# A four-layer gated transformer on one core: the next norm's centred input summed in PSUM at the ends of the attention layers, and the mixture's gate moved into its one-hots

## The reference, cut to what matters

```
x = x + tanh(g_xattn[0]) * L0_xattn(layernorm(x), ctx)      # differential attention, output Wp, bias bp
x = x + tanh(g_ffn[0])   * L0_ffn(layernorm(x))             # 8 experts, top 1, gate = softmax probability
x = x + tanh(g_xattn[1]) * L1_xattn(layernorm(x), ctx)      # linear attention, output Wo, bias bo
x = x + tanh(g_ffn[1])   * L1_ffn(layernorm(x))             # token-shift mixing: sigmoid(r) * (relu(k)^2 W_v)
x = x + tanh(g_xattn[2]) * L2_xattn(layernorm(x), ctx)      # masked softmax attention
x = x + tanh(g_ffn[2])   * L2_ffn(layernorm(x))             # shared expert + 8 routed, top 2
x = x + tanh(g_xattn[3]) * L3_xattn(layernorm(x), ctx)      # softmax attention, rows masked at the end
x = x + tanh(g_ffn[3])   * L3_ffn(layernorm(x))             # sparse heads + dense causal heads
```

## Time and profile before

| what | value |
|---|---|
| median of 3 runs | 517.68 us (516.72 to 518.56) |
| profiled execution, its own time | 518.73 us |
| its span in the trace | 516.6 us |
| PE busy | 454.9 us, 88% of the span |
| DVE, ACT, POOL busy | 277.6, 231.3, 94.7 us |
| chain that ended last | PE 67%, DVE 17%, ACT 9%, nothing shown 4% |
| mean granted TensorE clock | 0.973 of full |

### The profile page before, as it was taken

One profiled execution on the slowest core, in us unless ns is written; L12 is line 12 of the kernel. 1 busy time (PEld: TensorE's weight loads), 2 busy tenths in 40 slices (PEclk: granted clock), 3 DMA queues, 4 the chain that ended last, 5 costly groups with the idle time before them and its releaser, 6 DMA issues.

```text
span 516.6 us, 6960 instructions
## 1 busy us (share of the span) xinstructions
PE 454.9 (88%) x2690; PEld 257.6 (50%) x2690; DVE 277.6 (54%) x567; ACT 231.3 (45%) x447; POOL 94.7 (18%) x87
## 2 busy tenths in 40 slices
PE   5889999889898887787888998889879979989996
PEld 2334443463773332576644774433346465566563
DVE  1566774344225446587216663546595568357451
ACT  3345565320331465534443335445664554547261
POOL 3000000140601002244000000003355314152300
PEclk9899999979999999899979999999997999999999
DMA  8500000530000000000000002001001101011000
GB/s 351 242 2 1 1 1 1 194 120 0 0 1 1 2 0 0 1 1 2 0 0 2 0 1 81 1 0 22 7 15 20 22 1 22 3 20 22 20 1 22
DMA packets 4594, 15.54 MB, mean 30 GB/s; under 512 B 1361, under 2 KB 1618, under 8 KB 4050
## 3 DMA queue, kind: packets, MB, share of 16 engines
q1 hardware_dynamic: 4562, 15.10, 8.7%
HBM read 12.73 MB, written 0.52 MB: 26 GB/s over the span
## 4 chain that ended last, share of the span: by engine, by line
PE 67%; DVE 17%; ACT 9%; issue 4%; POOL 1%; DMA 1%; SPq 0%; DVEq 0%; POOLq 0%
PE PS L503 58%; PE PS L1201 2%; DVE mxd L2285 2%; PE PS L736 2%; ACT xc L1407 1%; DVE mx L1846 1%; DVE wmoe L1839 1%; ACT xc L1408 1%; DVE keys L1993 1%; POOL wmoe L2510 1%; PE PS L574 1%; DMA cst<-const_dram 1%; DVE yb L2323 1%; DVE hp L1797 1%; ACT wmoe L1699 1%
## 5 line engine op out<-in xcount | busy, mean ns | idle before, releaser
L503 PE MATMUL PS<-PTB,keys 128*64 128x128 f32 (+4 forms) x416 | 46.1, 401 | 0.1
L1711 ACT COPY PTB<-PS 128x768 f32<-128x768 f32 (+1 forms) x24 | 20.9, 872 | 34.6 <-PE PS L1201 34.3
L1993 DVE TENSOR_REDUCE keys<-PS 128x9 f32<-128x693 f32 x32 | 26.6, 874 | 10.8 <-PE PS L503 10.8
L503 PE MATMUL PS<-keys,PTB 32*128 32x231 f32 (+2 forms) x384 | 29.6, 348 | 3.0 <-DVE keys L1968 1.6
L503 PEld LDWEIGHTS PS<-PTB,keys 128*64 128x64 f32 (+3 forms) x416 | 22.5, 148 | 17.9 <-issue 14.1
L503 PE MATMUL PS<-x,cst 128*128 128x512 f32 x32 | 19.5, 711 | 13.4 <-DMA cst<-const_dram 5.9
L2510 POOL TENSOR_TENSOR wmoe<-wmoe,mx 128x616 f32<-128x616 f32 x16 | 19.5, 1216 | 63.1 <-DVE mx L1848 63.1
L2528 POOL TENSOR_TENSOR den<-den,cst 128x1024 f32<-128x1024 f32 x7 | 16.9, 2421 | 76.4 <-DMA den<-wmoe 76.4
L503 PEld LDWEIGHTS PS<-keys,PTB 32*128 32x128 f32 (+1 forms) x384 | 21.2, 190 | 17.7 <-issue 12.8
L1532 ACT ACTIVATE PT<-PS 116x512 f32<-116x512 f32 (+1 forms) x32 | 17.4, 597 | 23.5 <-PE PS L503 23.5
L503 PE MATMUL PS<-wmoe 64*128 64x512 f32 (+3 forms) x128 | 24.1, 474 | 4.2 <-ACT mask L1699 3.1
(11 more groups left out here) (346 smaller groups left out, 976.5 us busy)
## 6 DMA issues: line engine op xcount, KB each, us to landing
wmoe<-w_dram SPq DMA_DIRECT2D x2, 2048.0 KB, 11.8
den<-wmoe SPq DMA_DIRECT2D x28, 64.0 KB, 2.3
wa<-wa_dram SPq DMA_DIRECT2D x4, 256.0 KB, 5.2
wlate<-ew_dram SPq DMA_DIRECT2D x2, 512.0 KB, 4.6
wd<-wd_dram SPq DMA_DIRECT2D x1, 1024.0 KB, 8.4
wlate<-wm_dram SPq DMA_DIRECT2D x1, 1024.0 KB, 4.7
cst<-const_dram SPq DMA_DIRECT2D x1, 738.0 KB, 6.5
cst<-const_dram SPq DMA_DIRECT2D x1, 670.5 KB, 4.6
```

The costliest lines, as they stand in the source:

```text
L503: return nc.tensor.matmul(o, l, r, start=start, stop=stop, skip_group_check=True)
L1711: nc.scalar.copy(PTR[n % 2][:, :, 0:width], PS[:, 4:6, 0:width]).then_inc(S("d_turned"), 1)
L1993: last = v.tensor_reduce(mxn[:, 2 * half + t, :].rearrange("p (g r) -> p g r", r=32)[:, :, 12:15], PS[:, 0:NG, t * 256:t * 256 + GK].rearr ...
```

## The change

The sum of the old x and the gated projection is formed inside the centring product. For six norms, (1, half 1), (3, both), (5, half 1) and (7, both), `ln_centre` is replaced by two products into one bank: `join_x` multiplies the old x by `center` and leaves the sum open, and `join_att` adds the product of `att` with a matrix `WC` that holds the output matrix, centred over its output features and multiplied by the gate. What the output bias contributes is a column `CENTRED_BIAS`, which ACT adds inside the square and DVE inside the scale; in layer 3 POOL adds it (masked) to x ahead of time, the mask is applied when `att` is placed, and the residual is one DVE operation that reads the projection's bank. The old path (projection, bias on ACT, add on DVE) stays for x itself, behind the join. The four `WC` matrices are made on DVE, three operations each, the first in `gates` of layer 0 and three in the expert loop, and PE centres three bias columns with one-column products.

The mixture's gate is multiplied with tanh(g_ffn[0]) in one 128x8 operation and then into every one-hot, so that `moe_add` is one DVE operation in place of two. Several orders are rewritten: in `between` on PE, ACT and DVE, at the end of `attention3`, and at the beginning of `final_layer`. Five `keep_clock` groups are gone.

```diff
--- before.py
+++ after.py
@@ banks and numbering @@
-BETWEEN = [("query", 0), ("den", 0), ("num", 0), ("project", 0), ("query", 1), ("k", 0), ("den", 1), ("num", 1),
...
+BETWEEN = [("query", 0), ("den", 0), ("num", 0), ("project", 0), ("k", 0), ("query", 1), ("r", 0), ("den", 1),
...
+        WC = [wa0[:, 0, :]] + [ctxf[:, 128 * n:128 * n + 128] for n in range(3)]
@@ PE @@
+            def join_x(i, b):
+
+                if i > 1:
+                    pe.wait_ge(S(f"x_ready_{b}"), i - 1)
+                mm(PS[:, centre_bank(i, b), :], C("center"), xb[b], stop=False)
+
+            def join_att(i, b):
+                mm(PS[:, centre_bank(i, b), :], WC[i // 2], att[:, b, :], start=False).then_inc(S(f"ln_centered_{b}"), 1)
@@ PE, end of layer 0 @@
                 ln_variance(1, 0)
                 keep_clock(2, 512, 512)
                 turn(1)
-                keep_clock(2, 512)
+                pe.wait_ge(S("centred"), CENTRED["first"])
+                join_x(1, 1)
                 project(1)
-                keep_clock(2, 512, 512)
-                pe.wait_ge(S("st_y_placed"), B)
@@ PE, attention of layer 2 @@
                 ln_centre(i + 1, 0)
                 step()
+                join_x(i + 1, 1)
                 ln_variance(i + 1, 0)
@@ PE, attention3 @@
                 for u in range(NU3):
+                    if u == 3:
+                        turn(0)
                     turned_scores(u)
                     if u + 1 < NU3:
                         scores(u + 1, 1)
+                    if u == 3:
+                        pe.wait_ge(S("st_att_done"), FIRST["att_done"] + 1)
+                        join_att(7, 0)
                     if u > 0:
                         turn_sums(u - 1)
                     if u + 1 < NU3:
                         turn_max(u + 1)
                     if u + 2 < NU3:
                         scores(u + 2, 0)
+                    if u == 2:
+                        pe.wait_ge(S("l3_set"), 8 + 2)
+                        join_x(7, 0)
                     if u == 3:
-                        turn(0)
-                        keep_clock(ROW_BANKS[0], 512)
-                        project(0)
+                        project3(0)
                     weigh(u)
-                ln_centre(7, 0)
+                ln_variance(7, 0)
                 turn_sums(NU3 - 1)
-                ln_variance(7, 0)
+                pe.wait_ge(S("l3_set"), 8 + 4)
+                join_x(7, 1)
                 turn(1)
-                keep_clock(KEY_BANKS[0], 512)
-                project(1)
+
+            def project3(b):
+                mm(PS[:, PROJECT_BANKS[b], :], wa3[:, 3, :], att[:, b, :]).then_inc(S("st_projected"), 1)
@@ PE, moe @@
                 for b in range(B):
-                    if b == 0:
-                        ln_centre(1, 1)
-                    else:
+                    if b == 1:
                         ln_variance(1, 1)
@@ PE, between @@
                 lin_sums(0)
+                join_x(3, 0)
                 combine(6, 1)
                 combine(7, 1)
+                pe.wait_ge(S("lin_att"), 1)
+                join_att(3, 0)
+                ln_centre(2, 1)
+                ln_variance(3, 0)
                 lin_project(0)
-                ln_centre(2, 1)
-                ln_centre(3, 0)
                 ln_variance(2, 1)
-                ln_variance(3, 0)
-                keep_clock(5, 512)
+                arrived(pe, "wf1")
+                pe.wait_ge(S("lin_y"), 1)
+                mixed(0, 1, 4)
                 lin_query(1)
-                arrived(pe, "wf1")
-                mixed(0, 1, 4)
+                mixed(0, 0, 0)
                 lin_sums(1)
-                mixed(0, 0, 0)
                 mix_values(0, 1)
+                join_x(3, 1)
+                pe.wait_ge(S("lin_att"), 2)
+                join_att(3, 1)
                 lin_project(1)
                 ln_centre(4, 0)
-                ln_centre(3, 1)
+                ln_variance(3, 1)
                 ln_variance(4, 0)
-                ln_variance(3, 1)
                 pe.wait_ge(S("at_k_placed"), 1)
                 query2(0, 0, 4)
                 query2(0, 1, 5)
+                pe.wait_ge(S("lin_y"), 2)
                 mixed(1, 1, 6)
@@ PE, final_layer @@
                 prepare(0)
-                pe.wait_ge(S("st_y_placed"), FIRST["y_placed"] + B)
                 pe.wait_ge(S("pool_set"), POOL_SET["swap"])
+                pe.wait_ge(S("st_att_done"), FIRST["att_done"] + B)
                 for j in (1, 0):
                     mm(PS[:, 2 + j, :], wswap[j], h[0]).then_inc(S("d_swapped"), 1)
+                join_att(7, 1)
+                project3(1)
                 prepare(1)
-                ln_centre(7, 1)
+                ln_variance(7, 1)
                 router(0)
-                ln_variance(7, 1)
                 scores(0)
+                pe.wait_ge(S("x_ready_1"), 7)
                 tokens(0)
@@ ACT @@
             def ln_squares(i, b):
                 act.wait_ge(S(f"ln_centered_{b}"), i + 1)
-                A_(sq[:, b, :], PS[:, centre_bank(i, b), :], ACT.Square).then_inc(S(f"ln_sq_{b}"), 1)
+                at = CENTRED_BIAS.get((i, b))
+                plus = {} if at is None else dict(bias=small[:, at:at + 1])
+                A_(sq[:, b, :], PS[:, centre_bank(i, b), :], ACT.Square, **plus).then_inc(S(f"ln_sq_{b}"), 1)
@@ ACT, between @@
                 lin_shares(0)
+                ln_squares(3, 0)
+                ln_squares(2, 1)
+                ln_root(3, 0)
                 lin_project(0)
-                ln_squares(2, 1)
-                ln_squares(3, 0)
                 ln_root(2, 1)
-                ln_root(3, 0)
-                lin_shares(1)
                 act.preload_act_table_set(TANHS)
                 mix_gate(0, 0)
                 act.preload_act_table_set(ROOTS)
+                lin_shares(1)
+                ln_squares(3, 1)
+                ln_squares(4, 0)
+                ln_root(3, 1)
+                ln_root(4, 0)
                 lin_project(1)
-                ln_squares(4, 0)
-                ln_squares(3, 1)
-                ln_root(4, 0)
-                ln_root(3, 1)
                 place2(0, 0, 4)
@@ DVE @@
+                    last = v.scalar_tensor_tensor(h[b], centred_x, small[:, at:at + 1], xc[:, b, :], ALU.add, ALU.mult)
+                last.then_inc(S(f"ln_h_{b}"), 1)
+
+            def centred(n, w, gate):
+
+                link(v.tensor_reduce(small[:, n:n + 1], w, AX.X, ALU.add))
+                link(v.tensor_scalar(small[:, n:n + 1], small[:, n:n + 1], -1.0 / D, None, ALU.mult))
+                v.tensor_scalar(WC[n], w, small[:, n:n + 1], tg[:, gate:gate + 1], ALU.add, ALU.mult).then_inc(S("centred"), 1)
@@ DVE, attention3 @@
                 def place(b):
                     dve.wait_ge(S("st_turned"), FIRST["turned"] + b + 1)
-                    v.tensor_copy(att[:, b, :], PS[:, MAX_BANK, :]).then_inc(S("st_att_done"), 1)
+                    v.tensor_tensor(att[:, b, :], PS[:, MAX_BANK, :], mask3f[:, b * T:(b + 1) * T],
+                                    ALU.mult).then_inc(S("st_att_done"), 1)
 
                 def add(b):
-                    dve.wait_ge(S("st_y_placed"), FIRST["y_placed"] + b + 1)
-                    link(v.tensor_tensor(yb[:, b, :], yb[:, b, :], mask3f[:, b * T:(b + 1) * T], ALU.mult))
-                    residual(b, 3)
+                    dve.wait_ge(S("st_projected"), FIRST["projected"] + b + 1)
+                    dve.wait_ge(S("l3_set"), 8 + 2 * (b + 1))
+                    v.scalar_tensor_tensor(xb[b], PS[:, PROJECT_BANKS[b], :], tg[:, 3:4], xb[b], ALU.mult,
+                                           ALU.add).then_inc(S(f"x_ready_{b}"), 1)
...
                 add(0)
                 take(NU3 - 1)
+                ln_scale(7, 0)
                 place(1)
-                ln_scale(7, 0)
                 add(1)
@@ DVE, start, moe and between @@
+                dve.wait_ge(S("gates"), 1)
+                dve.wait_ge(S("lam_dots"), 2)
+                v.tensor_scalar(small[:, 8:9], PS[:, 4, 400:401], tg[:, 0:1], None, ALU.mult)
+                link(v.tensor_scalar(r8t[:, 6, :], r8t[:, 6, :], tg[:, 4:5], None, ALU.mult))
...
+                    if 1 <= e <= 3:
+                        centred(e, (wa1, wa2, wa3)[e - 1][:, 3, :], e)
+                    elif e == 4:
+                        dve.wait_ge(S("moe_slots"), 3)
+                        v.tensor_scalar(small[:, 9:10], PS[:, 3, 256:257], tg[:, 1:2], None, ALU.mult)
+                        v.tensor_scalar(small[:, 10:11], PS[:, 3, 257:258], tg[:, 2:3], None, ALU.mult)
+                        v.tensor_scalar(small[:, 11:12], small[:, 13:14], tg[:, 3:4], None, ALU.mult).then_inc(S("centred"), 1)
-                v.tensor_scalar(GC[b][e % 2], destb[:, b * T:(b + 1) * T], C("slotid")[:, e:e + 1], None,
-                                ALU.is_equal).then_inc(S("moe_GT"), 1)
+                tokens = slice(b * T, (b + 1) * T)
```

(21 more changed lines are left out.)

60 lines of the change are left out of this document (37 added, 23 removed).

## The result

The changed kernel takes 522.77 us in the median of 20 executions (517.78 to 527.82), the kernel before 518.5 in the median of 20 (516.72 to 521.66). That is 4.3 us or 0.8% between the medians. The ratios in this document leave out executions that took over 1.5% more than the fastest of their kernel (5 of the 20 of the change), and the median of what is left is called trimmed. The trimmed median of the change is 521.35, its ratio 1.006 with a 95% interval of 1.0037 to 1.0082: slower by 0.6%. The forecast was 517.4, with a range of 514.7 to 520.1. The profiled execution is one of the slower ones of the 20, 526.37 us by its own time at a mean clock of 0.953, where the 20 together had 0.961.

A forecast was written before the change was run, and what follows sets the result against it. PE was taken to bound the kernel (busy 454.9 of 516.6 us), so edits count only where PE waits. Terms +0.6 - 1.94 + 0 + 1.84 - 0.24 - 0.5 = -0.24 took the median from 517.68 to 517.4, range 514.7 to 520.1.

The forecast's parts named there:

- Start of layer 0, +0.6: Start of layer 0: an added small DVE operation and `centred(0)` ahead of the reductions cost +0.6 us (0.2 to 1.1).
- the other +0.17: Start of layer 0: one more small DVE operation ahead of the eight at 14.91 costs +0.17 us with its gap.
- The half-clock rival: Ahead of layer 2's queries: 2.86 us of PE idle time brings half clock, price 1.5 to 3 us, time 519.5; chance 0.22.
- the sign that it named: The page's slice at 194 to 200 us shows a clock below 0.8.
- End of layer 0, -1.94: End of layer 0, norm (1, 1): the join replaces the projection, the DVE and ACT detour goes, variance 1.94 us earlier.
- The mixture, 0: Expert loop: longer one-hots and added DVE work are covered by DVE's idle time, 0 us (-0.1 to +0.2).
- `between`, +1.84: Between layers 1 and 2: product k 2.0 us earlier, but queueing makes the first layer-2 query 1.84 later (+0.5 to +2.5).
- The load's drain: Between layers 1 and 2: a drain makes each ACT table switch 2.66 us, sum 0.5 higher, time 517.9; chance 0.03.
- Norm 5, -0.24: End of layer 2: the join of norm (5, 1) changes the time by -0.24 us (-1.0 to +0.6).
- Layer 3, -0.5: End of layer 3: `prepare(0)` at 346.3 instead of 349.42, half 1's add later, first final-layer scores -0.5 us (-2.6 to +0.8).
- The sum, -0.24: Whole kernel: all terms together give -0.24 us, profiled execution 518.5, median 517.4.

The follow-up runs named there:

- x1: The changed kernel with `centred(0)`, which makes the first WC matrix, moved behind the squares of half 1 at the end of layer 0: 517.38 us.
- x5: The kernel before plus the three DVE operations of the first centred matrix, in the changed kernel's place, result unread: 523.10 us against 519.06.
- x9: The changed kernel with unread products filling PE's wait ahead of the second group's turned maxima at the start of layer 0: 518.55 us.
- x3: The changed kernel with half 1's shares put ahead of both table loads and its division ahead of the mixing add, between layers 1 and 2: 520.94 us.
- x7: The edits of x1 and x3 together on the changed kernel: 516.23 us.
- x6: x1 with the phase between layers 1 and 2 (norm 3 of both halves, orders of PE, ACT, DVE) as in the kernel before: 514.29 us.
- x10: The kernel before with the join of norm (1, 1) alone, its WC matrix made late: 515.23 us against 519.25.
- x4: The kernel before with the mixture's gate in the one-hots and nothing else: 518.96 us against 518.90.
- x11: x1 with all joins of norm 3 kept, but norm 4 of half 0 put ahead of norm 3 of half 1: 514.74 us, ratio 0.9917.
- x12: x6 with the end of layer 2, norm (5, 1), as in the kernel before too: 515.24 us against 514.29.
- x2: The changed kernel with seven unread products in PE's waits between layers 1 and 2: 531.55 us.

## Why the prediction was wrong

- **Start of layer 0, +0.6.** This step failed. Its serial size was right (+0.53 at the reductions against +0.43, and under 0.05 for the other +0.17), but the prediction took the delay for the whole price: "less the 0.32 of slack, +0.43". What the runs showed in its place: it lengthens PE's wait from 0.98 to 1.47 us at a place where the clock then drops to 1.2 GHz, for 3 to 24 us in the four traces, over work in which PE is nearly always busy (11.11 of 12 us in 33 to 45, in the change), so that nearly half of the stretch is lost. In the change's trace that was 4.76 us. Price in the medians 4 to 5.4 us, 2 to 4 between the trimmed ones (x1 against the change, x5 against before, x9 against the change).
- **The half-clock rival** had the mechanism and the wrong wait. It looked at 2.86 us ahead of the query (found: 2.54, and in this execution half clock behind it, the sign that it named). That wait did not decide: x3 and x7 have it with full clock behind it, and x6, which is without it, has the same mean clock as x1 (0.974). Against itself the rival held "the 2.78 at the end of layer 0, whose centring has the usual 1.10". That was a misreading: 2.78 is the distance between the starts of two rows, not a wait. Behind the projection (92.49 to 93.62) stood four records that nobody reads, up to 95.33, so that PE was not idle ahead of the centring at 95.27:

```profile
...
93.45 1.88 PE L503 MATMUL PS<-cst 128*128 128x512 f32 x4
...
```

  The wait that decided was a shorter one, and the prediction never asked this question of the start of layer 0.
- **End of layer 0, -1.94.** Right: -1.89 in the timeline of x10, -1.90 in that of the change.
- **The mixture, 0.** Right: x4.
- **`between`, +1.84.** Right in size (+1.70 between the traces of x6 and x1; k to query 17.1 forecast, 16.85 found) and in its parts: x11 brought the query 2.59 nearer to k by turning round the order that the step named.
- **The load's drain.** The shares started 0.02 behind the second load's end. No drain is seen on either side of the load, which itself starts 0.02 behind the gate's end, and the Trainium skill's ("ScalarE: Activation LUTs", "What ACT_TABLE_LOAD costs") 2.66 us a switch isn't borne out by this trace; its 1.28 us for the load is.
- **Norm 5, -0.24.** Not contradicted (x12), and too small to be settled by these runs.
- **Layer 3, -0.5.** Right: -0.42 in the traces. The add of half 1 waited for the projection, as the step said, 5.43 behind `prepare(0)` (forecast 5.5), and `prepare(0)` came 2.53 earlier (forecast 3.1).
- **The sum, -0.24.** Without norm 5 the traces give +0.53 - 1.90 + 0 + 1.70 - 0.42 = -0.09, so the serial part of the forecast held. That x1 then measures 517.38, next to the 517.4 forecast, is luck in part: it leaves out the 0.43 of this sum, and the median of 12 executions that differ by 5 us is no sharper than that. The range failed because the clock was given one place and one size (1.5 to 3 us), where the runs show a spread of 10 us over 20 executions of one kernel. The distances forecast for the changed profile came out (the scale 2.53 behind the variance), the absolute times did not: product k was forecast 3.3 earlier than before and came 2.35 later.

What stays open: why a wait of about 1.5 us at 33 brought half clock in every trace that had it, while one of 2.54 ahead of the first layer-2 query did so in the change and in x1 and not in x3 and x7; why x10 gained in the clock as well as in the work; and what sets how long a half-clock stretch lasts (3.4 us in x3, 10 in the change, 20 and more in x2 and x5).

## What to carry to other kernels

A short addition to an engine that is idle half the time can cost several times its length, if PE waits for it right ahead of a long stretch of dense PE work: read the granted clock by windows over every place where an edit lengthens a wait of PE, even by half a microsecond, and not only at the longest waits. Work that is needed late should be made late: three operations moved by 60 us turned +0.6% into -0.4%. A distance between the starts of two rows is not a wait: look at what the engine does in between. And tell work from clock by the distance between two rows with the same clock in both traces, where there are such. The mean of time x granted clock is a first hint, rough to about 1 us.

## What the runs showed of the hardware

The same kernel ran 517.78 to 527.82 us, and its mean granted clock went from 0.970 to 0.951 with it; time x clock stayed between 501.3 and 505.5. A wait of PE of 0.97 or 0.98 us at 33 had full clock behind it in eleven traces, one of 1.46 to 1.58 us half clock in four of four, for 3.4 to 23.9 us, and the same delay with the wait filled by unread products (1.56 us in the trace) full clock again. Half clock over dense PE work made that work longer by a little under half of the stretch (4.8 us for 10.2, 11.1 for 23.9). Between the layers seven unread products removed the neighbouring falls in the profiled execution and left the mean clock where it was. The best kernels of this study, x6 and x11, take 514.29 and 514.74 us, 0.8% under the kernel before.
